# Two edits behind a scan: the last four expert tiles are reordered on ScalarE and TensorE, and GpSimd takes every second multiply of a layer norm's gain from VectorE

## The reference

```python
x = x + mamba(xn) + experts(xn)

def mamba(x):                     # 16 states per channel, a scan over 1024 steps
    ... dt, B, C from x ...
    h = h * exp(dt * A) + (dt * x) * B
    y = sum(h * C) + x * D;  out = (y * silu(gate)) @ W_out + b_out
    return layernorm(out + x) * ln_g + ln_b

def experts(x):                   # 8 experts, the best 2 of each token
    h = gelu(layernorm(x @ w1 + b1) * ln1_g + ln1_b)
    y = h @ w2 + b2;  out = sum over the two experts of weight * y
    return layernorm(out + x) * fln_g + fln_b
```

## Time and profile before

| what | us |
|---|---|
| median of 3 runs | 1719.26 (1716.1 to 1726.77) |
| the profiled execution, its own time | 1718.58 |
| its span, first to last instruction | 1716.8 |
| the scan ends, the seven tiles' steps begin | about 1522 |
| last `copy_y` ends | 1592.5 |
| last instruction | 1716.8 |

### The profile page before, as it was taken

One profiled execution on the slowest core, in us unless ns is written; L12 is line 12 of the kernel. 1 busy time (PEld: TensorE's weight loads), 2 busy tenths in 40 slices (PEclk: granted clock), 3 DMA queues, 4 the chain that ended last, 5 costly groups with the idle time before them and its releaser, 6 DMA issues.

```text
span 1716.8 us, 27483 instructions
## 1 busy us (share of the span) xinstructions
PE 1514.6 (88%) x6796; PEld 936.6 (55%) x6796; DVE 1512.5 (88%) x2462; ACT 1285.0 (75%) x2433; POOL 1002.3 (58%) x585
## 2 busy tenths in 40 slices
PE   5998469999999999999999898989899999997887
PEld 4665135655555555655556565656555555654332
DVE  6777489999999999999999999999999999963896
ACT  3555368787878887887878787878888888766687
POOL 2777746666666656575656575656666666642234
PEclk9677779999999999999999999999999999998899
DMA  7999832333433343333433433433333433452794
GB/s 233 355 295 354 286 114 73 100 91 100 112 92 100 93 113 88 100 89 99 104 99 92 112 87 101 107 94 94 100 92 97 105 89 88 115 131 38 240 295 158
DMA packets 178472, 228.38 MB, mean 133 GB/s; under 512 B 45967, under 2 KB 145048, under 8 KB 178331
## 3 DMA queue, kind: packets, MB, share of 16 engines
q1 hardware_dynamic: 137422, 166.02, 31.8%
q0 software_dynamic: 25584, 35.54, 11.1%
q10 hardware_dynamic: 15328, 25.20, 4.4%
HBM read 146.17 MB, written 80.53 MB: 132 GB/s over the span
## 4 chain that ended last, share of the span: by engine, by line
DVE 34%; PE 22%; ACT 15%; issue 14%; ACTq 3%; POOL 1%; DMA 1%; DVEq 0%; POOLq 0%; SPq 0%
DVE area L1460 7%; PE psX L1097 5%; DVE area L1473 5%; DVE area L1469 4%; PE psY L1118 4%; DVE area L1490 3%; DVE more L1525 3%; ACT area L705 3%; ACT h_T L742 3%; PE psH L1083 2%; PE psT L1145 2%; ACTq L726 2%; PE psT L1175 2%; PE psT L1069 2%; ACT L747 1%
## 5 line engine op out<-in xcount | busy, mean ns | idle before, releaser
L586 POOL TENSOR_TENSOR area<-area,more 128x1024 f32<-128x1024 f32 x256 | 600.0, 2361 | 481.7 <-DVE area L1469 246.1
L1490 DVE TENSOR_TENSOR area<-area,psD 128x1024 f32<-128x1024 f32 x256 | 310.3, 1212 | 0.3 <-issue 0.3
L1083 PE MATMUL psH<-w_sb,ffn_xT 128*128 x524 | 255.7, 611 | 44.8 <-DVE area L1504 38.9
L570 POOL DMA_INDIRECT expert_d<-y_out,meta x135 | 220.9, 1636 | 77.8 <-ACT y_out L721 48.1
L1118 PE MATMUL psY<-ident,area 128*128 128x128 f32 x2048 | 252.4, 277 | 0.0
L1118 PEld LDWEIGHTS psY<-ident,area 128*128 128x128 f32 x2048 | 223.8, 142 | 13.4
L705 ACT ACTIVATE area<-area,A_sb 128x512 f32<-128x512 f32 x256 | 170.0, 712 | 80.2 <-DVE area L1473 43.5
L1097 PE MATMUL psX<-w_sb,h_T 128*128 x720 | 180.3, 394 | 13.1 <-issue 10.4
L699 ACT ACTIVATE psD<-area,A_sb 128x512 f32<-128x512 f32 x256 | 174.8, 683 | 11.1 <-POOL area L577 4.8
L1083 PEld LDWEIGHTS psH<-w_sb,ffn_xT 128*128 128x128 f32 x524 | 92.4, 192 | 146.2 <-issue 145.6
L557 POOL DMA_INDIRECT sorted_x<-area,place x128 | 128.0, 1000 | 72.7 <-issue 37.4
(11 more groups left out here) (236 smaller groups left out, 2721.2 us busy)
## 6 DMA issues: line engine op xcount, KB each, us to landing
more<-B_rows_d SPq DMA_DIRECT2D x128, 512.0 KB, 4.0
xin<-sorted_x SPq DMA_DIRECT2D x135, 128.0 KB, 2.5
area<-L_attn_x SPq DMA_DIRECT2D x8, 1024.0 KB, 6.4
xnT_d<-w_sb ACTq DMA_DIRECT2D x16, 512.0 KB, 6.8
expert_d<-area ACTq DMA_DIRECT2D x8, 1024.0 KB, 11.6
ssm_d<-w_sb ACTq DMA_DIRECT2D x16, 512.0 KB
w_sb<-L_ffn_w SPq DMA_DIRECT2D x16, 512.0 KB
more<-ssm_d SPq DMA_DIRECT2D x16, 512.0 KB, 3.8
```

What stands on the lines that cost most here:

```text
L570: pool.indirect_dma_start(out=expert_d, out_offset=bass.IndirectOffsetOnAxis(ap=meta_tok[:, t % RING, :], axis=0), in_=y_out[:, t % 2, :], ...
L586: pool.tensor_tensor(inflow[:, k], dtx, B_rep[par][:, k].rearrange("p (a t) -> p a t", a=1).to_broadcast([P, KD, CHUNK]), ALU.mult).then_i ...
L1083: nc.tensor.matmul(h_bank(t), ffn_xT[:, k, :], w1_sb[:, bass.ds(e, 1), k, :].rearrange("p o h -> p (o h)"), start=(k == 0), stop=False)
L1490: V.tensor_tensor(h, h, C_rep[k].rearrange("p (a t) -> p a t", a=1) .to_broadcast([P, KD, CHUNK]), ALU.mult).then_inc(S[f"hC{k}_done"], 1)
```

## The change

On ScalarE the two remaining `hidden_root` steps, of tiles f and last, go ahead of the Gelus of d and e. All four remaining tiles' Gelus then follow in one stretch with one table. The pair `with_exp`, `with_gelu` between them is gone. `copy_y(c)` goes ahead of `gelu(d)`. The four `root` steps that open the closing stage are split around `copy_y(f)`, and `normalise_sums(-3)` goes behind `copy_y(last)`. On TensorE `transpose_h(f)` goes ahead of `down(d)`.

In the closing stage `gains(i)` stays on VectorE for even i. For odd i (1, 3, ..., 27: 14 of 28 that have a Mamba half ahead) GpSimd does the same multiply, right behind its own multiply for the expert half. A new semaphore tells TensorE's `add_zero`.

```diff
             for i in range(PAIRS_E):
                 pool.wait_ge(S["e_norm"], i + END_LEAD + 1)
                 pool.tensor_tensor(er1[i % END_RING], er1[i % END_RING], gain1, ALU.mult).then_inc(S["e_gain1"], 1)
+                if i % 2 == 1 and i + END_LEAD < PAIRS_E:
+                    v = er0[(i + END_LEAD) % END_RING]
+                    pool.tensor_tensor(v, v, gain0, ALU.mult).then_inc(S["e_gain_pool"], 1)
...
             hidden_root(e)
             copy_y(b)
             take_out(CHUNKS, 1, psY[:, CHUNK:])
+            hidden_root(f)
             copy_xT(last)
+            hidden_root(last)
             with_gelu()
+            copy_y(c)
             gelu(d)
-            copy_y(c)
             gelu(e)
+            gelu(f)
+            copy_y(d)
+            gelu(last)
+            copy_y(e)
             with_exp()
-            hidden_root(f)
-            hidden_root(last)
-            copy_y(d)
-            with_gelu()
-            gelu(f)
-            copy_y(e)
-            gelu(last)
-            with_exp()
-            for i in range(-END_LEAD, 0):
-                root(i)
+            root(-4)
+            root(-3)
             copy_y(f)
-            for i in range(-END_LEAD, -2):
-                normalise_sums(i)
+            root(-2)
+            root(-1)
+            normalise_sums(-4)
             copy_y(last)
+            normalise_sums(-3)
             for i in range(-2, 0):
                 normalise_sums(i)
...
             down(c, last)
+            transpose_h(f)
             down(d)
-            transpose_h(f)
             transpose_h(last)
...
             def add_zero(p):
                 q = p % END_RING
-                pe.wait_ge(S["e_gain"], p + 1)
+                if p < END_LEAD:
+                    pe.wait_ge(S["e_gain"], p + 1)
+                elif p % 2 == 0:
+                    pe.wait_ge(S["e_gain"], END_LEAD + (p - END_LEAD) // 2 + 1)
+                else:
+                    pe.wait_ge(S["e_gain_pool"], (p - END_LEAD) // 2 + 1)
...
                     sums(i + 2)
-                if i + END_LEAD < PAIRS_E:
+                if i % 2 == 0 and i + END_LEAD < PAIRS_E:
                     gains(i)
```

More of the change, by code:

```diff
@@ L276, in build_program @@
             y_ready y_copied y_stored pool_consts pick_ready scattered_last
-            e_bias e_chain e_var e_ln e_root e_scale e_norm e_gain e_gain1 e_zero e_sum""".split()
+            e_bias e_chain e_var e_ln e_root e_scale e_norm e_gain e_gain_pool e_gain1 e_zero e_sum""".split()
         names += [f"{n}{q}" for n in ("e_done", "e_store") for q in range(END_BUFS)]
@@ L611, in _ @@
             pool.wait_ge(S["w_end"], 16 * len(end_loads))
+            gain0 = e_g0.rearrange("p (o d) -> p o d", o=1).to_broadcast([P, 2, DIM])
             gain1 = e_g1.rearrange("p (o d) -> p o d", o=1).to_broadcast([P, 2, DIM])
```

## The result

| | before | changed |
|---|---|---|
| median of 22 runs each, us | 1719.36 (1714.01 to 1726.77) | 1725.3 (1718.93 to 1735.21) |
| ratio, 95% interval | | 1.0033 [1.0020, 1.0046] |
| the profiled execution, its own time | 1718.58 | 1719.56 |
| its span | 1716.8 | 1717.8 |

What follows compares the result with a forecast made beforehand. It took a chain of waits to bound the expert tiles, and a nearly full VectorE and DMA the closing stage, with two-tile reads colliding with GpSimd's. 1718.58 - 3.1 (tiles) + 8.5 (closing stage) = 1724.0 us; range 1712 to 1731.

Steps and rivals of the forecast that it cites:

- The reading of the expert tiles as a chain of waits: Expert tiles' end: no engine full; `down`, `copy_y`, next `down` follow each other, 5.35 us per tile.
- The reading of the closing stage: Closing stage: VectorE busy 14.69 of 15 us, DMA share 0.98; two-tile VectorE instructions and GpSimd's multiplies do not run together.
- Clock and copies: Expert tiles: TensorE's clock falls at about 1571.4, `down(e)` half slow; last `copy_y` at 1589.4, not 1592.5: gain 3.1 us.
- the two durations taken from the earlier trace: Expert tiles: TensorE's clock stays low for 9.8 or 6.8 us, so full speed returns between 1578.2 and 1581.2.
- the ends of -1.2 and 5.8: Expert tiles: loss of 1.2 us if the clock stays low throughout, gain of 5.8 if it never falls.
- What follows moves along whole: Behind the last `copy_y`: the 3.1 us gain passes on undiminished; VectorE's 2.53 us DMA wait hides the extra `normalise_sums`.
- The closing stage: In odd turns `scales` waits for GpSimd's second multiply, 0.66 us each; loss 7.9 to 9.2 us, taken as 8.5.
- Leaving the odd multiply out gives 0.31 per odd turn: Closing stage: without VectorE's odd multiply `scales` waits only for the root; 14 x 0.31 = 4.3 us gained.
- the first rival: Closing stage: VectorE gets the port between GpSimd's two multiplies; gain 2.0 to 4.3 us, whole 1712.4; chance 0.17.
- the slower case: Closing stage: TensorE's clock falls, 2.3 us per fall; from six falls 1738 us and over; chance 0.04.
- The expert tiles gave something: Answers the rival that the expert tiles give nothing: clock low through the last `down`, +1.2 us, whole 1729.0; chance 0.15.
- VectorE as the real limit: Closing stage: the offload gives the full 14.1 us, whole 1701.4 us; chance 0.02.

Runs made afterwards that it cites:

- experiment 3: Kernel before with only the closing-stage edits, but GpSimd's second multiply replaced by three memsets of the same tile; one execution, 1732.37 us.
- experiment 2, odd_left_out: Kernel before with only the closing-stage edits, but the odd Mamba-half multiplies done by no engine; 1785.57 us, ratio 0.9999 to the kernel before.
- tiles_only: Kernel before with only the new order of expert tiles, none of the closing-stage edits; 1784.04 us, ratio 0.9990 to the kernel before.
- after_skip: Changed kernel without tile e's scatter into `expert_d`; one execution, last scatter 20.80 us behind `copy_y(c)`, in the changed kernel 22.71.
- before_skip: Kernel before without tile e's scatter into `expert_d`; one execution, last scatter 24.45 us behind `copy_y(c)`, in the kernel before 24.50.
- closing_only: Kernel before with only GpSimd's 14 multiplies in the closing stage, expert tiles unchanged; 1792.49 us, ratio 1.0036 to the kernel before.
- held: Kernel before with GpSimd's expert-half multiply delayed to run beside VectorE's statistics, and `copy_out` a turn later; 1717.0 us, ratio 0.9971 to the kernel before.
- held_tiles: Kernel before with GpSimd's multiply delayed beside the statistics, `copy_out` a turn later, and the changed order of tiles; 1775.21 us, ratio 0.9979.
- held_tiles2: As `held_tiles`, with `down(d)` ahead of `transpose_h(f)` and `copy_y(d)` ahead of `gelu(f)`; 1770.82 us, ratio 0.9953; measured again 1782.02 us, 0.9970.

## Why the prediction held, and where it did not

**What bounds the kernel.** The reading of the expert tiles as a chain of waits was right up to `copy_y`. The reading of the closing stage was half right: the two-tile reads collide with GpSimd's (experiment 3), but VectorE's full queue was not what set the turn (experiment 2).

**Clock and copies: right, a little pessimistic.** The clock fell at the idle time for which it was forecast (3.08 us; forecast about 3.2), and `down(d)` took 3.78 (3.73). The fall lasted 6.8 us, the shorter of the two durations taken from the earlier trace rows. But it began about 0.8 us ahead of the transposes of f, within the idle time, where the forecast let it begin with them, and the transposes came 9.3 us behind `copy_y(b)`, not 9.9. So `down(e)` was at full speed and not half slow. Hence 4.82 us for the last `copy_y`, where 3.1 was taken, inside the ends of -1.2 and 5.8. The two durations were too few: before's own trace has a third fall, of 3.4 us, at `down` of last (a mean of 0.72 from 1587 to 1593), and the changed order had one as short in `tiles_only`.

**"What follows moves along whole": this step failed.** It was one sentence, for what the root and DMA behind the last copy do; it looked at what comes after the last scatter and not at the scatters' own pace. The numbers lay in before's trace: the last scatter landed in 3.72 us, and the forecast's own full-speed cycle of 3.61 is shorter than that. At that cycle the next scatter must wait. Of 4.82 us, 3.3 were given back there (3.19 in the last scatter's start, 0.15 in its landing). `after_skip` and `before_skip` show that the scatters were the limit. So 1.5 arrived in place of 3.1.

**The closing stage: the mechanism right, its size 1.3 us too large.** Forecast: `scales` about 1.1 us, ending with GpSimd's second multiply; measured 1.11, ending within 0.01. Forecast 0.66 per odd turn for twelve of them, 7.9, and 0 to 0.66 for each of turns 1 and 27. Measured: eleven steps of 0.63, 6.9, and 0.3 for the twelfth; turns 1 and 27 cost nothing, where half was taken. The whole lost 7.2 (7.3 between `closing_only` and `tiles_only`), under the lower end of 7.9.

**A side step failed.** "Leaving the odd multiply out gives 0.31 per odd turn" (4.3 us) was measured as 0, since the even multiply grew by 0.32 (0.78 to 1.10). It was never a term of the sum, but it was the prize in the first rival and with it that rival's time was too low.

**The rivals.** The second multiply did not slip past: of 14 `scales` only the last was not held. TensorE's clock stayed up once the closing stage was under way (PEclk 1.00 with TensorE 12.79 of 15 us busy), so the slower case did not occur. At the start of the stage there was one fall, 10.2 us long where before's was 6.8 (a mean of 0.66 from 1594 to 1609, against 0.66 from 1604 to 1614), but the `scales` there came no later behind the first load. The 5.91 of 11.3 us with which that rival argued is TensorE's work in a window that holds the fall itself, and so says little on what led to it. The expert tiles gave something, if less than their copies. VectorE as the real limit is excluded by `odd_left_out`. And the sentence in the first rival that two turns could shrink by only 2% before transfers bind was wrong: `held` shrank them by 4.6% (7.15 to 6.82). A DMA share of 0.98 in one window was not a hard stop.

**The sum.** 1718.58 - 1.48 + 7.18 = 1724.3, against 1718.58 - 3.1 + 8.5 = 1724.0 forecast. The gain was 1.6 us too large and the loss 1.3 too large. That they cancel to 0.3 is luck; that the closing stage's loss outweighs the tiles' gain is not.

## What to carry to other kernels

Before work is moved off a busy engine, leave it out altogether and look at the time: if nothing comes, as here, handing the same work to another engine has nothing to win, and the engine that gets it can still cost. Where a producer is made faster, compare its new cycle with the slowest serial step behind it, DMAs that wait for each other among them, and not only with the last consumer. And where the reads of two engines hold each other off, their place within the turn can matter more than which of the two does the work. Before the traces of two kernels are compared over a fraction of a microsecond, compare TensorE's clock in them.

## What the runs showed of the hardware

- `scales`, asking 0.17 us after GpSimd's second multiply had begun, waited for the end of all of it (1.11 us for 4 elements per partition, instead of 0.15). Beside memsets of the same tile it took 0.16. No run shows who is first when VectorE already waits at the end of GpSimd's first multiply.
- A scatter that adds 128 rows of 256 f32 to `expert_d` took 3.8 to 4.1 us to land in the changed kernel's chain, and when each waits for the one before, 0.71 more until the next starts.
- The changed order of tiles had TensorE's clock at half for 6.8 us in one execution and for 3.4 in two others (`tiles_only`, `held_tiles`), at the same idle time of 3.08 us. One kernel, `held_tiles2`, had 6.8 in one execution and 3.4 in the other, and its first load moved by 1.2 us. What sets the length was not tried.
- Two executions of the same unchanged stages, of before and of the changed kernel, lay 4.7 us apart at `copy_y(b)`, nearly the size of the whole effect.
